# A graph network on one core: kept tables, scaling by inverse sums and PSUM copies are divided anew among VectorE, GpSimd and ScalarE

## What is computed

```python
h = relu(layernorm(x))
x = x + gat(h)          # attention: sums of weighted neighbours / their sum of weights, + bias
h = relu(layernorm(x))
x = x + gcn(h)          # two graph convolutions, then a dense layer on [h, x1, x2]
```

## Time and profile before

| what | time, us |
|---|---|
| median of 3 runs | 8650.75 (8644.58 to 8668.01) |
| span of the profiled execution | 6959.5 |
| middle stage within the span (first VectorE instruction to the last tile finished) | 2614.4 to 2803.8 |
| VectorE busy in the span | 3523.0 (51%) |
| ScalarE busy | 2073.8 (30%) |
| GpSimd busy | 4908.5 (71%) |
| TensorE busy | 4805.8 (69%) |

### The profile page before, as it was taken

How to read it: one execution, slowest core, us unless ns; L and a number is a source line. 1 busy time by engine, 2 the same in 40 slices (tenths; PEclk the granted TensorE clock), 3 DMA queues, 4 the chain that set the end, 5 groups by cost and what they waited for, 6 DMA issues and landing times. The chain is left out here.

```text
span 6959.5 us, 113181 instructions
## 1 busy us (share of the span) xinstructions
PE 4805.8 (69%) x27409; PEld 3529.7 (51%) x27410; DVE 3523.0 (51%) x8745; ACT 2073.8 (30%) x5831; POOL 4908.5 (71%) x4806
## 2 busy tenths in 40 slices
PE   2699999999999994555555555556666666666655
PEld 1466666666666664344444444445544544444443
DVE  6688888888888888222222222223222222222224
ACT  3567777777777774000000000001000000000001
POOL 1777777776776756677777777774677777777775
PEclk9899999999999997555555555555555555555555
DMA  6777776777776655211111111111211111111115
GB/s 207 250 210 211 210 215 207 211 212 212 212 213 210 209 175 158 82 52 52 51 52 52 51 52 51 52 51 43 53 33 34 34 33 34 34 34 33 33 26 161
DMA packets 515795, 783.25 MB, mean 113 GB/s; under 512 B 143367, under 2 KB 392452, under 8 KB 514956
## 3 DMA queue, kind: packets, MB, share of 16 engines
q0 software_dynamic: 176176, 377.82, 21.0%
q1 hardware_dynamic: 303390, 369.82, 16.6%
q10 hardware_dynamic: 35758, 30.37, 1.4%
HBM read 695.07 MB, written 82.51 MB: 112 GB/s over the span
## 5 line engine op out<-in xcount | busy, mean ns | idle before, releaser
L1690 POOL DMA_INDIRECT c_g<-conv_table,c_idx x3128 | 3010.6, 962 | 1128.3 <-issue 952.9
L1767 PE MATMUL c_sums<-c_g,acc 128*128 x7040 | 1976.1, 441 | 1714.2 <-SPq L1653 1077.4
L1767 PEld LDWEIGHTS c_sums<-c_g,acc 128*128 128x128 f32 x7040 | 1626.4, 322 | 2220.1 <-issue 2210.1
L1002 POOL DMA_INDIRECT acc<-gat_table,ga_idx x1564 | 1615.8, 1033 | 653.0 <-issue 458.2
L1731 DVE TENSOR_TENSOR acc<-acc,c_sums 128x128 f32 (+1 forms) x1760 | 448.5, 255 | 2838.1 <-PE c_sums L1767 2821.7
L1386 PE MATMUL ga_sums<-ga_wg,ga_S 128*128 128x265 f32 x3520 | 999.3, 406 | 7.1 <-DVE ga_wg L1260 6.0
L1336 PE MATMUL ga_dstp<-ga_oht,ga_h 128*128 128x256 bf16 x5280 | 729.9, 275 | 76.0 <-DVE ga_prod L1181 69.7
L1386 PEld LDWEIGHTS ga_sums<-ga_wg,ga_S 128*128 128x128 f32 x3520 | 610.4, 193 | 171.4 <-issue 65.3
L1336 PEld LDWEIGHTS ga_dstp<-ga_oht,ga_h 128*128 128x128 bf16 x5280 | 505.7, 98 | 344.4 <-DVE ga_prod L1181 130.1
L1181 DVE SCALAR_TENSOR_TENSOR ga_prod<-acc,ga_a_dst,ga_dstp 128x512 f32<-128x512 f32 x880 | 645.0, 733 | 8.0 <-issue 6.7
L1077 ACT ACTIVATE ga_S<-iota_row,ga_dcol 128x128 f32<-128x128 f32 x1760 | 605.0, 392 | 73.5 <-issue 70.6
(11 more groups left out here) (253 smaller groups left out, 3731.5 us busy)
## 6 DMA issues: line engine op xcount, KB each, us to landing
ga_h<-h_parts SPq DMA_DIRECT2D x880, 192.0 KB
ga_dl<-dl_rows SPq DMA_DIRECT2D x110, 512.0 KB
c_g<-conv_table,c_idx POOLq DMA_INDIRECT x3128, 2.5
acc<-gat_table,ga_idx POOLq DMA_INDIRECT x1564
h_parts<-h_split SPq DMA_DIRECT2D x14, 1344.0 KB, 5.2
gat_table<-h_out SPq DMA_DIRECT2D x14, 952.0 KB
x_rows<-md_x SPq DMA_DIRECT2D x14, 896.0 KB, 7.1
fc_x<-x_rows ACTq DMA_DIRECT2D x98, 128.0 KB
```

Of the source, the lines that this page charges most:

```text
L1002: pool.indirect_dma_start(G[:, (v * PC + j) * HROW:(v * PC + j + 1) * HROW], None, gat_table, bass.IndirectOffsetOnAxis(idx[:, c:c + 1], 0 ...
L1690: pool.indirect_dma_start(G[:, c % (2 * SLOTS), :], None, table, bass.IndirectOffsetOnAxis(idx[:, c:c + 1], 0)).then_inc(rows_in[c // 2 % ...
L1767: last = nc.tensor.matmul(sums[:, b % R, 0:width], S[:, u * CH + 2 * b + j, :], flat[:, bass.ds(slots[b] * (2 * width) + j * width, width) ...
```

## The change

In `dense_phase` reciprocal deviation and shift are written straight into tables with a column for each tile, the kept ones where `keep` is given and new ones otherwise; the two copies (L536, L537) go, and so does the wait that guarded the two small buffers. In `mid_phase` VectorE multiplies by the inverse sums (`share`): group 0 before the rest of the sums of weights is inverted, group g + 1 at the head of `pre` of group g. GpSimd only adds the bias. ScalarE copies tiles 0 to 5 of each group, VectorE tile 6. In three places the reason to leave out the bounds check is gone, so that the check is made while running: ScalarE's awaited values in `gat_phase` (the new `counts`), `load_frees`, and TensorE's awaited values in `conv_phase`.

```diff
@@ dense_phase
-    rstd = [sb(ctx, f"{name}_rstd{u}", [P, GT]) for u in range(2)]
-    shift = [sb(ctx, f"{name}_shift{u}", [P, GT]) for u in range(2)]
+    if keep is None:
+        keep = [sb(ctx, f"{name}_{n}", [P, TILES]) for n in ("rstd", "shift")]
+    rstd, shift = ([t[:, g * GT:(g + 1) * GT] for g in range(GROUPS)] for t in keep)
@@ normal(g)
-                u = g % 2
                 dve.wait_ge(s_sd, g + 1)
-                if g >= 2:
-                    dve.wait_ge(relu_done, GT * (g - 1))
-                link(nc.vector.reciprocal(rstd[u][:, :], sd[:, :]))
-                nc.vector.scalar_tensor_tensor(shift[u][:, :], mv[:, :, 0], -1.0, rstd[u][:, :], ALU.mult, ALU.mult).then_inc(s_norm, 1)
+                link(nc.vector.reciprocal(rstd[g], sd[:, :]))
+                nc.vector.scalar_tensor_tensor(shift[g], mv[:, :, 0], -1.0, rstd[g], ALU.mult, ALU.mult).then_inc(s_norm, 1)
                 dve.wait_ge(s_norm, g + 1)
-                if keep:
-                    nc.vector.tensor_copy(keep[0][:, g * GT:(g + 1) * GT], rstd[u][:, :])
-                    nc.vector.tensor_copy(keep[1][:, g * GT:(g + 1) * GT], shift[u][:, :])
@@ gat_phase
+        def counts(tab, eng, low, high):
+
+            _, regs = nc.values_load_multi_w_load_instructions(tab, engines=[eng], min_val=low, max_val=high)
+            return regs
...
-                            registers(row_tab[u][0:1, 1, :], mybir.EngineType.Activation, READY + 1, READY + 1 + UNITS // PB))
+                            counts(row_tab[u][0:1, 1, :], mybir.EngineType.Activation, READY + 1, READY + 1 + UNITS // PB))
@@ mid_phase
             nc.vector.tensor_scalar(dinv[:, :], acc[:, :, S0], 1.0, None, ALU.add).then_inc(deg_ready, 1)
+            dve.wait_ge(den_ready, 1)
+            share(dve, 0)
             link(nc.vector.tensor_scalar(dens(1, GROUPS), dens(1, GROUPS), 1e-10, None, ALU.max))
             nc.vector.reciprocal(dens(1, GROUPS), dens(1, GROUPS)).then_inc(den_ready, 1)
+            dve.wait_ge(den_ready, 2)
...
                 heads = columns(g)[:, :, :, 1:HCOLS]
-                den = columns(g)[:, :, :, 0:1]
-                if g < 2:
-                    pool.wait_ge(den_ready, g + 1)
-                nc.gpsimd.tensor_tensor(heads, heads, spread(den, [[WROW, GT], [HCOLS, HEADS], [0, HDIM]]), ALU.mult).then_inc(scaled, 1)
                 pool.wait_ge(scaled, g + 1)
                 nc.gpsimd.tensor_tensor(heads, heads, spread(bias[:, :], [[0, GT], [HDIM, HEADS], [1, HDIM]]), ALU.add).then_inc(attended, 1)
 
+        def share(dve, g):
+
+            heads, den = columns(g)[:, :, :, 1:HCOLS], columns(g)[:, :, :, 0:1]
+            nc.vector.tensor_tensor(heads, heads, spread(den, [[WROW, GT], [HCOLS, HEADS], [0, HDIM]]), ALU.mult).then_inc(scaled, 1)
+
         def pre(dve, g, xg):
+            if g + 1 < GROUPS:
+                share(dve, g + 1)
             dve.wait_ge(attended, g + 1)
...
-                    lambda pe: pe.wait_ge(s_w, 32), pre=pre, keep=x1_norm, finish_act=finish_act, by_act=(1, 3, 5), hold=hold, at_end=at_end,
+                    lambda pe: pe.wait_ge(s_w, 32), pre=pre, keep=x1_norm, finish_act=finish_act, by_act=(0, 1, 2, 3, 4, 5), hold=hold, at_end=at_end,
@@ load_frees
-    _, regs = nc.values_load_multi_w_load_instructions(
-        row, engines=[eng], min_val=USED, max_val=USED + UNITS,
-        skip_runtime_bounds_check_because="unit numbers are clamped where they are worked out")
+    _, regs = nc.values_load_multi_w_load_instructions(row, engines=[eng], min_val=USED, max_val=USED + UNITS)
@@ conv_phase, TensorE's second read
-                        need_row[0:1, bass.ds(m * UL, UL)], engines=[mybir.EngineType.PE], min_val=READY + 1, max_val=READY + 1 + UNITS,
-                        skip_runtime_bounds_check_because="pair numbers are clamped where they are worked out")
+                        need_row[0:1, bass.ds(m * UL, UL)], engines=[mybir.EngineType.PE], min_val=READY + 1, max_val=READY + 1 + UNITS)
```

More of the change, by code:

```diff
@@ L575, in relu @@
                     act.wait_ge(turn_done, GT * (g - NH) + a + 1)
-                nc.scalar.activation(hn[g % NH][:, a, :], xg[g % NX][:, a, :], ACT.Relu, bias=shift[g % 2][:, a:a + 1],
-                                     scale=rstd[g % 2][:, a:a + 1]).then_inc(relu_done, 1)
+                nc.scalar.activation(hn[g % NH][:, a, :], xg[g % NX][:, a, :], ACT.Relu, bias=shift[g][:, a:a + 1],
+                                     scale=rstd[g][:, a:a + 1]).then_inc(relu_done, 1)
             def copy(n):
```

## The result

The median of four runs after the change is 8772.04 us (8754.25 to 8789.62), beside 8659.38 for four of the kernel before in the same set of runs: ratio 1.0127, 95% interval 1.0099 to 1.0154. It is slower, by 113 us; 8610 was forecast, and the range ended at 8655.

The account below looks back on a forecast made before the run. Gathers were taken to bound the convolutions, and VectorE and GpSimd taking turns the middle stage's first regime. Gain 47.6 - 1 (TensorE) - 2 (loads) - 4 (checks) = about 40 us; 8650.75 - 40 = 8610, range 8595 to 8655.

Parts of the forecast that it names:

- The checks: Bounds checks made while running, in attention and convolutions: mostly hidden, 4 us lost, ends 0 and 60.
- GpSimd's checks: GpSimd's 49 sets of checks: up to 64 us, set against 110.9 us of waiting for VectorE's release.
- Slower: ScalarE's checks: Rival, attention slot 3: checks hold up rectifications behind the read, 1.3 us an iteration, 143 us lost, 8750; chance 0.10.
- Start: Middle stage's beginning, groups 0 and 1: group 2 starts at 2640.3 instead of 2654.26, 14 us earlier.
- Each later group: Middle stage, groups 2 to 13 on VectorE: period 8.65 us, group 13 starting 47.6 us earlier.
- GpSimd goes first: Rival, middle stage: GpSimd's addition precedes VectorE's L1484, period 11.8 us, gain about 6 us, 8645; chance 0.10.
- ScalarE: Middle stage: six copies and its other work take 6.9 to 8.0 us a group, inside the 8.65 us period.
- TensorE: Middle stage: at half clock up to 11.4 us a group until the clock rises; 1 us lost.
- SP and queues: Middle stage loads: same transfers in the same order, 8.2 us a group; 2 us lost, bounds 0 and 6.
- The other dense stage: Only loses the wait for its small buffers; its shift still takes turns with GpSimd; costs nothing.
- The sum against the span: Whole kernel: gain summed against the 6959.5 us span; the median's extra 1691.25 us taken as unchanged.

Follow-up runs that it names:

- e2_checks_alone: Kernel before with only the bounds checks added, dense stages as before; 7090.51 us, ratio 1.0206 to the kernel before.
- r0_after: The changed kernel, unaltered, run again in another set beside the kernel before; 8804.67 us against 8674.57, ratio 1.0146.
- e6_tables_alone: Changed kernel with values raised to zero instead of checked, GpSimd multiplying again, ScalarE copying three of seven tiles; 8679.05 us, ratio 1.0015 to the kernel before.
- e7_three_copies: Changed kernel with values raised to zero instead of checked and ScalarE making three of seven copies instead of six; 8553.54 us, ratio 0.9984 to before.
- e9_clamps_again: Changed kernel with every checked value raised to zero instead, rerun at the slower pace; 8537.41 us, ratio 0.9973 to the kernel before.
- e1_clamps: Changed kernel with every checked value raised to at least zero instead of checked, faster pace; 6908.3 us beside 6949.57 before, ratio 0.9939.

## Why the prediction was wrong

*The checks* is the step that failed. It took 4 us, with 60 as the upper end, and they cost 141 at the faster pace (e2_checks_alone) and about 170 at the slower (r0_after is 125.6 us above e6_tables_alone, though its middle stage is 45 us shorter). The signs that the prediction named for it are there: in e2_checks_alone L1453 starts at 2721.6 us instead of 2614.4, and the gap before the one-hot pair is 2.47 us. Three things in the step were wrong.

- The argument "its work is two quanta ahead of VectorE" looked at the rectifications alone. The next instruction behind the read is the one-hot pair, with 0.39 us of margin (median) to TensorE's sum. What stands behind the read was looked up for the wrong consumer. This was 84 us at the faster pace and about 110 at the slower.
- "From above three register operations a value, 1.3 us for eight" was no upper end. A check is 147 + 18 ns, eight take 1.8 us.
- "TensorE's and SP's checks stand in the convolutions, where gathers set the pace", so nothing: they cost some 30 us at the faster pace and 52 at the slower. That GpSimd's stream is the bound did not shield it: at the slower pace it waits for slots that others give back, and at the faster its gathers got longer, for a reason that stays open.

*GpSimd's checks* cost 25 us at the faster pace, where the prediction let waits of 110.9 us cover them, and none that shows at the slower.

*The rival "Slower: ScalarE's checks"* was right, at a chance of 0.10: it named the place and the turning point of 0.4 us an iteration, and priced it at 1.3 us with all of it passing on, 8750. What passed on is 84 / 110 = 0.76 us and 112 / 110 = 1.02 us of 1.8. It had the rectifications as carrier, not the one-hot pair. That its 8750 is near the measured 8772 is in part luck: it took 143 us for ScalarE's checks, which cost 112 there, and nothing for those of TensorE and SyncE, which cost 52.

*Start* was 12.2 us for 14. *Each later group* was right: period 8.52 for 8.65. That group 13 comes at 121.3 us after L1453 for 121.1 is closer than the steps were, since 1.8 us lost at the start and eleven times 0.13 gained cancel. VectorE went first each time, as argued from the earlier trace rows, and *GpSimd goes first* did not happen: it would have shown as an L1490 of 5.6 us. The sum of that rival was wrong besides: 34.7 and 6 us off the forecast's 40 leave no gain, 8650, and not 6 us. The Trainium skill's page "SBUF — State Buffer", section "SBUF: two separate sides", says that the pair of ports is held for a whole instruction and that the other engine waits meanwhile; this trace agrees. GpSimd's addition contains 5.40 - 3.66 = 1.74 us of waiting for L1490, and epsilon 0.34 of waiting for GpSimd, forecast as 0.45.

*ScalarE* (11.11 us busy of 14) stayed inside the period and *TensorE* was granted 0.78 at 26 to 40 us into the stage, 1.00, its upper level, at 64 to 78, and between 0.88 and 0.96 in three later stretches. *SP and queues*: one late load, 0.91 us, for 2 forecast. *The other dense stage*: nothing to see. The copies that moved to ScalarE were costed as 1.0 us a group and were worth 2.2 (10.77 - 8.57, e7_three_copies); the list of a group had the short wait for the root already, so its sum did not suffer.

*The sum against the span*: 1691 us were taken "as unchanged" on top of it. They were a slower pace within the stages: attention is some 1090 us longer, the two gather streams together some 530 (e9_clamps_again against e1_clamps). A rest of a fifth of the time that no view explains should have widened the range.

## What to carry to other kernels

A check of a loaded value is not free on the engine that loads it: about 0.225 us a value, in a row, with all behind it waiting; count what stands directly behind it and its margin, the smallest one, not the engine's mean lead. A burst like this costs by its place: spread, the same checks gave back 112 us at the slower pace, all of ScalarE's price that shows there, and behind the instruction with the short margin instead of ahead of it they left none there either; at the faster pace 18 to 20 of 84 us stayed. If the check is wanted, it should be put there first. A raise to zero cost nothing that could be seen at the faster pace, but it is no check: it lets through a value above the upper bound, and one between zero and the lower.

When a wait sits inside an instruction, taking the instruction away moves the wait; what shortens the stage is to take away the other holder (2 against 21 us here).

## What was not expected of the hardware

The same kernel, its instructions and its transfers unchanged, took 6950 us in some sets of runs and 8560 to 8675 in others. Attention is 2300 us at the one and 3390 at the other, a convolution's stream 1965 to 1989 and 2238 to 2248, the middle stage 142 at both (e1_clamps and e9_clamps_again, the same kernel). What sets the pace is open. It is not TensorE's granted clock, 0.695 and 0.696 over the two spans, and not the time of the transfers themselves: the packets of the largest queue took some 1470 and 1480 us of the 16 engines' time. What differs is short operations of the sequencers. A check on TensorE's sequencer, in e2_checks_alone and then in after (min/median/max ns):

```profile
L1762 PEldq FUSED_REGOPS  x1966: 46/146/165, 2922.6 to 6986.5; - x197
```

```profile
L1762 PEldq FUSED_REGOPS  x1966: 2/146/1414, 3976.3 to 8657.0; - x197
```

The median is the same, but at the slower pace some take up to 1.4 us. In e9_clamps_again 315 of 3932 such operations of TensorE and 159 of 2263 register moves of SyncE last over 0.5 us; in e1_clamps none does. Whether that is the cause of the slower pace or a sign of it, and whether more operations on these two sequencers cost more there for this reason, was not tried.

A price seen at one pace need not be there at the other: GpSimd's checks and the moved read cost 25 and 18 to 20 us at the faster and nothing visible at the slower, TensorE's and SyncE's together 30 and 52.
